# Two-layer attention, gating and scan kernel: normalising on ScalarE, gates by tanh, output rows in chunks, new orders

## The reference, cut to what matters

```python
x = x + attn0(xn) + ffn0(xn)
xn = layernorm(x)
# state-space block, 256 inner channels, 16 states
xs, z = split(xn @ W_in)
xs = silu(causal_conv4(xs) + conv_b)
dt = softplus(xs @ W_dt + b_dt);  Bs = xs @ W_x
h  = h * exp(-A * dt) + Bs            # a scan over the tokens, 16 states
y  = (sum_over_states(h) + D * xs) * silu(z)
x1 = y @ W_out
# feed-forward, 512 hidden
h = silu((xn @ w1.T) * w1_s) * ((xn @ w2.T) * w2_s)
h = gelu((h @ h1.T) * h1_s);  h = gelu((h @ h2.T) * h2_s)
x = x + x1 + (h @ w3.T) * w3_s
```

## Time and profile before

| | |
|---|---|
| runs (3) | 415.56, 415.57 (median), 419.93 us |
| profiled execution | 414.44 us, span 412.5 us |
| granted TensorE clock, mean | 0.983 |
| busy: PE, PEld | 385.6 us (93%), 195.0 us (47%) |
| busy: DVE, ACT, POOL | 302.4 us (73%), 320.5 us (78%), 239.1 us (58%) |
| POOL acc additions, line 1115, x128 | 158.2 us |
| DVE scans, line 1076, x128 | 145.7 us |
| ACT exponentials of line 1019, x128 | 81.6 us |
| chain that ended last | PE 53%, ACT 22%, DVE 13%, issue 9% |

### The profile page before, as it was taken

How to read it: one execution, slowest core, us unless ns; L and a number is a source line. 1 busy time by engine, 2 the same in 40 slices (tenths; PEclk the granted TensorE clock), 3 DMA queues, 4 the chain that set the end, 5 groups by cost and what they waited for, 6 DMA issues and landing times.

```text
span 412.5 us, 5932 instructions
## 1 busy us (share of the span) xinstructions
PE 385.6 (93%) x1864; PEld 195.0 (47%) x1864; DVE 302.4 (73%) x509; ACT 320.5 (78%) x537; POOL 239.1 (58%) x276
## 2 busy tenths in 40 slices
PE   7999999999998999898869898999999999889995
PEld 6875454545544353342213443545446544375445
DVE  5857869687696979226847998788997799978500
ACT  2331668686689868999999999999999999959510
POOL 5233642351423210134398797699997899998640
PEclk9999999999999999999977999999999999989999
DMA  5189556576255220000000000000000000000000
GB/s 188 50 143 196 116 151 151 101 180 100 68 85 113 30 50 2 3 0 2 0 1 0 1 2 0 0 2 25 1 1 2 0 26 1 0 2 25 1 0 27
DMA packets 27679, 19.03 MB, mean 46 GB/s; under 512 B 2816, under 2 KB 26240, under 8 KB 27392
## 3 DMA queue, kind: packets, MB, share of 16 engines
q1 hardware_dynamic: 27648, 18.65, 21.1%
HBM read 13.46 MB, written 4.98 MB: 45 GB/s over the span
## 4 chain that ended last, share of the span: by engine, by line
PE 53%; ACT 22%; DVE 13%; issue 9%; DMA 1%; POOL 1%; SPq 0%; ACTq 0%; POOLq 0%; DVEq 0%
PE bank L852 7%; PE bank L840 6%; DVE hb L1076 6%; PE bank L352 5%; ACT da L1019 5%; PE bank L337 4%; PE bank L323 4%; PE bank L391 3%; PE bank L383 3%; PE bank L911 3%; ACT pt L519 3%; PE bank L445 3%; DVE mx L558 2%; PE bank L829 2%; PE bank L830 2%
## 5 line engine op out<-in xcount | busy, mean ns | idle before, releaser
L1115 POOL TENSOR_TENSOR acc<-acc,hb 128x512 f32<-128x512 f32 x128 | 158.2, 1267 | 35.3 <-DVE hb L1076 25.2
L1076 DVE TENSOR_TENSOR_SCAN hb<-da,bank 128x512 f32<-128x512 f32 x128 | 145.7, 1200 | 32.3 <-PE bank L813 28.7
L558 DVE TENSOR_REDUCE mx<-bank 128x2 f32<-128x512 f32 x128 | 82.5, 682 | 27.1 <-PE bank L323 21.6
L519 ACT ACTIVATE pt<-bank 128x512 f32<-128x512 f32 x128 | 71.0, 597 | 17.3 <-PE bank L337 16.6
L1019 ACT ACTIVATE da<-dt,nega 128x510 f32<-128x510 f32 x128 | 81.6, 710 | 0.2
L852 PE MATMUL bank<-gelu,ld 128*128 128x512 f32 x128 | 58.4, 595 | 2.1 <-ACT gelu L1000 2.1
L840 PE MATMUL bank<-sil,ld 128*128 128x512 f32 x128 | 60.0, 604 | 0.0
L337 PE MATMUL bank<-q_st,k_st 51*128 51x512 bf16 x128 | 43.4, 388 | 5.6 <-ACT pt L519 5.6
L323 PE MATMUL bank<-k_st,q_st 48*128 48x256 bf16 x256 | 43.4, 273 | 2.4 <-DVE mx L558 2.0
L852 PEld LDWEIGHTS bank<-gelu,ld 128*128 128x128 f32 x128 | 23.7, 190 | 30.5 <-issue 26.0
L840 PEld LDWEIGHTS bank<-sil,ld 128*128 128x128 f32 x128 | 24.2, 194 | 27.3 <-issue 26.2
(11 more groups left out here) (132 smaller groups left out, 565.1 us busy)
## 6 DMA issues: line engine op xcount, KB each, us to landing
q_st<-q_scr SPq DMA_DIRECT2D x8, 384.0 KB, 6.3
q_st<-q_scr SPq DMA_DIRECT2D x15, 192.0 KB, 3.9
ld<-in_pack SPq DMA_DIRECT2D x2, 1024.0 KB, 5.6
q_scr<-qk_parts SPq DMA_DIRECT2D x8, 192.0 KB, 2.3
k_st<-k_scr SPq DMA_DIRECT2D x15, 96.0 KB, 4.9
q_scr<-qk_parts SPq DMA_DIRECT2D x8, 128.0 KB, 1.9
out<-x SPq DMA_DIRECT2D x4, 256.0 KB, 2.0
ld<-in_pack SPq DMA_DIRECT2D x1, 968.0 KB, 5.6
```

The lines of the kernel that those rows point to most:

```text
L519: act(pt[:, n % 8, :], st(b, n)[:, :], ACT.Exp, scale=HD ** -0.5).then_inc(p_ok, 1)
L558: eng.tensor_reduce(mx[:, 2 * pair:2 * pair + 2, q], s_bank[n % 2][:, :].rearrange("p (h k) -> p h k", h=2), AX.X, ALU.max).then_inc(mx_ok, 1)
L1076: eng.tensor_tensor_scan(hb[:, s % NPAIR, c, :], da(n).rearrange("p b n -> p (b n)"), b_bank(g, s)[:, :], 0.0, ALU.mult, ALU.add).then_inc ...
L1115: TT(acc[:, g % 2, c, :], acc[:, g % 2, c, :], hb[:, s % NPAIR, c, :], ALU.add).then_inc(add_ok, 1)
```

## The change

Eight edits go together.
- Layer 0 and layer 1 normalise in one ScalarE pass, x * inverse + (-mean * inverse); VectorE makes the product -mean * inverse (`nmr`, `nmean`) after the inverse. Layer 0's `normalised` moves from VectorE to ScalarE. Epsilon is the bias of the square root.
- GpSimd's `biased` adds two tiles at a time.
- `start_acc` moves from ScalarE to GpSimd, one piece for each half.
- silu(u) = u/2 * (1 + tanh(u/2)): z's gate in all four groups (`TANH_Z`), x's gate and the feed-forward's in group 0 only (`TANH_X`, `TANH_FFN`). ScalarE takes tanh, VectorE multiplies by u (`zm`, `xm`, and a second operation in `mul`). The halves go into copies of the constants (`d_half`, `f1_half`, `f12_half`, `wout_half`), made in `decay_rates`, and into the scales of `b_in` and `dt`.
- `out` accumulates the y part of all four token tiles first, then one chunk of the feed-forward product at a time, each with a wait for its own `hid`.
- In the last group the output rows lie in both banks; residual and store are halved in all groups.
- The lists of all five queues are new. SP issues x ahead of the weights.
- 13 of the 96 warm blocks come after the first `A`.

```diff
 deviation0(k):
-    eng.wait_ge(st_mv, 2 * k + 2)
-    act(std[:, lo:hi], t["veps"][:, lo:hi], ACT.Sqrt).then_inc(st_sd, 1)
+    eng.wait_ge(st_mv, k + 1)
+    act(std[:, lo:hi], mv[:, lo:hi, 1], ACT.Sqrt, bias=t["eps"][:, 0:1]).then_inc(st_sd, 1)
+normalised(b):                                   # on ScalarE; VectorE's is removed
+    eng.wait_ge(st_rs, 2 * x_part(b) + 2)
+    reached(eng, xnT_ps, b - 1, 1, 1)
+    for q in range(TPB):
+        c = b * TPB + q
+        last = act(xn[:, q, :], x_sb[:, c, :], ACT.Identity, bias=nmr[:, c:c + 1], scale=rstd[:, c:c + 1])
+    last.then_inc(xn_ok, 1)
 inverse(k):                                      # and the same in layer 1
     eng.reciprocal(rstd[:, lo:hi], std[:, lo:hi]).then_inc(st_rs, 1)
+    eng.wait_ge(st_rs, 2 * k + 1)
+    eng.scalar_tensor_tensor(nmr[:, lo:hi], mv[:, lo:hi, 0], -1.0, rstd[:, lo:hi],
+                             ALU.mult, ALU.mult).then_inc(st_rs, 1)
 normalise(g):
-    act(xn[...], x1[:, c, :], ACT.Identity, bias=nmean[:, c:c + 1])     # four, then
-    act(xn[...], xn[...], ACT.Copy, scale=rstd[:, c:c + 1])             # four
+    act(xn[...], x1[:, c, :], ACT.Identity, bias=nmean[:, c:c + 1], scale=rstd[:, c:c + 1])
...
+TANH_Z, TANH_X, TANH_FFN = (0, 1, 2, 3), (0,), (0,)
 gate_z(g, c):
-    act(zs[:, g % 2, c, :], (pA, pB)[c][:, :], ACT.Silu).then_inc(z_ok, 1)
+    act(zs[:, g % 2, c, :], (pA, pB)[c][:, :], ACT.Tanh, scale=0.5).then_inc(z_ok, 1)
+z_mul(g, c):                                     # VectorE
+    reached(eng, z_ok, g, 2, c + 1)
+    STT(zs[:, g % 2, c, :], zs[:, g % 2, c, :], 1.0, (pA, pB)[c][:, :], ALU.add, ALU.mult).then_inc(zm_ok, 1)
+x_mul(g, c):                                     # VectorE, group 0
+    reached(eng, xs_ok, g, 2, c + 1)
+    STT(xs[:, g % 2, c, :], xs[:, g % 2, c, :], 1.0, xc[:, c, :], ALU.add, ALU.mult).then_inc(xm_ok, 1)
-start_acc(g):                                    # ScalarE
-    act(acc[:, g % 2, c, :], xs[:, g % 2, c, :], ACT.Copy, scale=t["D"][:, c:c + 1])
+start_acc(g, c):                                 # GpSimd
+    x_done(eng, g)
+    eng.tensor_scalar(acc[:, g % 2, c, :], xs[:, g % 2, c, :], d[:, c:c + 1], None, ALU.mult)
...
 out_rows:
-    for k in range(KC):
-        mm(pB[:, r], g3[:, k, r], w3[:, k, :], start=(k == 0), stop=False)
-    for c in range(CI):
-        last = mm(pB[:, r], y[:, c, r], wout[:, c, :], start=False, stop=(c == CI - 1))
+    n == 0: for q, c: mm(out_bank(g, q)[:, r], y[:, c, r], wo[:, c, :], start=..., stop=False)
+    n >= 1: reached(eng, g3_ok, g, KC, k + 1)
+            for q: mm(out_bank(g, q)[:, r], g3[:, k, r], w3[:, k, :], start=False, stop=...)
```

The orders' tails, as an example of how they differ (tensor):

```diff
-        out 2*b 3*second b 3*second b 2*second 2*b 8*third 4*out
+        ffn b ffn b out ffn b ffn b 2*b out out 3*second b 2*second b 2*second b second b 2*out third b 2*third
+        b third b 4*third 6*out
```

More of the change, by code:

```diff
@@ L120 @@
-    gpsimd="""ones 3*biased 8*G 2*qk_split maxima_split 6*G qk_split 2*G constants maxima_split 8*G qk_split maxima_split
-        8*G qk_split maxima_split 8*G qk_split maxima_split 8*G qk_split maxima_split 8*G maxima_split 8*G
-        maxima_split split 6*add split 26*add y 6*add y 13*add split 13*add y 5*add y 14*add split 20*add y
-        3*add y 22*add 2*y""",
+    sync="""x_in constants0 x_in head x_in ffn_weights 3*put fetch stack 3*put fetch put stack 2*put 3*rows fetch loads
+        2*put 3*rows loads put stack fetch rows put 2*rows put stack put fetch 3*rows stack 3*put fetch loads
+        3*rows stack 3*put fetch 3*rows 3*put fetch stack 3*rows stack 3*rows loads 8*out landed""",
@@ L124 @@
+    gpsimd="""ones 2*biased 8*G 2*qk_split maxima_split 8*G qk_split maxima_split 8*G biased maxima_split qk_split 8*G
+        maxima_split constants G qk_split 7*G maxima_split 3*G qk_split 5*G maxima_split qk_split 8*G
+        maxima_split 8*G maxima_split 2*start split 9*add 2*start 9*add split 13*add y 5*add y start 6*add start
+        8*add split 14*add y 4*add y 8*add start 3*add start 7*add split 11*add y 4*add y 26*add y add y""",
 )
@@ L949, in gate_z @@
             reached(eng, y_ok, g - 2, CI, CI)
-            act(zs[:, g % 2, c, :], (pA, pB)[c][:, :], ACT.Silu).then_inc(z_ok, 1)
+            if g in TANH_Z:
+                last = act(zs[:, g % 2, c, :], (pA, pB)[c][:, :], ACT.Tanh, scale=0.5)
+            else:
+                last = act(zs[:, g % 2, c, :], (pA, pB)[c][:, :], ACT.Silu)
+            last.then_inc(z_ok, 1)
         def gate_x(g, c):
@@ L954, in gate_x @@
             reached(eng, dt_ps, g - 2, 2, 2)
-            act(xs[:, g % 2, c, :], xc[:, c, :], ACT.Silu).then_inc(xs_ok, 1)
-        def start_acc(g):
-            reached(eng, xs_ok, g, 2, 2)
-            reached(eng, y_ok, g - 2, CI, CI)
-            for c in range(CI):
-                act(acc[:, g % 2, c, :], xs[:, g % 2, c, :], ACT.Copy,
-                    scale=t["D"][:, c:c + 1]).then_inc(acc_in, 1)
+            if g in TANH_X:
+                last = act(xs[:, g % 2, c, :], xc[:, c, :], ACT.Tanh, scale=0.5)
+            else:
+                last = act(xs[:, g % 2, c, :], xc[:, c, :], ACT.Silu)
+            last.then_inc(xs_ok, 1)
         def normalise(g):
@@ L1012, in decay @@
             if n == 0:
[L1013 removed]
+                settled(eng, i_act, NIA)
             if n == ND0:
@@ L1107, in gpsimd_pieces, with start_acc @@
         TT = eng.tensor_tensor
+        def start_acc(g, c):
+            x_done(eng, g)
+            reached(eng, y_ok, g - 2, CI, CI)
+            settled(eng, i_act, NIA)
+            d = d_half if g in TANH_X else t["D"]
+            eng.tensor_scalar(acc[:, g % 2, c, :], xs[:, g % 2, c, :], d[:, c:c + 1], None, ALU.mult).then_inc(acc_in, 1)
         def add(g, n):
@@ L1148, in constants @@
                               ALU.mult).then_inc(i_pool, 1)
-        return dict(constants=constants, split=split, add=lambda n: add(n // (2 * NS), n % (2 * NS)),
+        return dict(constants=constants, split=split, start=lambda n: start_acc(n // CI, n % CI), add=lambda n: add(n // (2 * NS), n % (2 * NS)),
                     y=lambda n: gated(n // CI, n % CI))
```

277 lines of the change are left out of this document (155 added, 122 removed).

## The result

The changed kernel takes 389.51 us (median of 5 runs, 389.35 to 391.72) against 415.57 us: 0.935 of the kernel before, 95% interval 0.9291 to 0.9408. The direction was right; the forecast had half of the size.

The account below looks back on a forecast made before the run. Start-up, then full TensorE in layer 0, then ScalarE from 160 us, with TensorE at the end, were taken to bound the kernel; -3.0 - 9.0 - 1.6 = -13.6 from 415.57 gives 402.0 us, own range 397 to 407, wider 394.5 to 410.

Parts of the forecast that it names:

- Start-up, -3.0: Kernel start up to the first scores: x issued first, epsilon as bias, normalising on ScalarE; 3.0 us sooner, ends 1 and 5.
- Layer 0, 0 us: Layer 0: ScalarE's added normalising hides behind full TensorE, and the 7.9 us taken off VectorE were in slack; no change.
- Head of layer 1, -3: Up to the second softplus: ScalarE's order has 113.4 against 116.2 us of work, so GpSimd's first addition comes 3 us sooner.
- -10.2: ScalarE between layer 0's fifth batch and layer 1's last x_out: 20 table loads instead of 28, 1.28 us each.
- The discount of 6 us for VectorE's products: ScalarE's stage: 14 new tanh-gate products on VectorE delay TensorE, taking 6 us off the 15.4 us gain.
- start_acc, -3.7 for three pairs: ScalarE's stage: three pairs of starting products leave ScalarE for GpSimd, -3.7 us; 0.8 us each on GpSimd, ends 0.6 and 1.27.
- ScalarE's stage -9.0: Layer 1, where ScalarE is full: fewer loads, start_acc moved, one-pass normalising, less VectorE's products; -9.0 us, ends -3 and -15.
- GpSimd sets the limit: First addition to y(5), group 2's second output product: GpSimd's work bounds the gain; y(5) near 347, span end near 397.
- Rival (a): GpSimd binds: starting product costs 1.27 us, its idle does not shrink, y(5) at 356, end at 408; chance 0.15.
- Rival (b): More comes back: ScalarE's whole 15.4 us and the stretch at clock 0.81; 397 us or lower; chance 0.12.
- Rivals (c) and (d): Tanh shares exp's table but not silu's or gelu's, 51 loads, 404.5, chance 0.08; or needs its own, 66 loads, 420, 0.06.
- Tail, -1.6: Kernel end: y part and first chunks run beside the last gelu, last residual and store halved; 1.6 us less.

## Why the prediction was right in direction and short in size

- **Start-up, -3.0, measured -5.0 at x_in together with layer 0.** The single steps came as written: first scores at 21.67 for "near 22", one pass of 0.88 us for 0.86 (only the small product ahead of it took 0.64 us for 0.2). The step that failed is "Layer 0, 0 us": VectorE is "rid of 7.9 us, also in slack". It is not in slack between the first scores and the first A: layer 0's normalising on VectorE costs 5.6 us, 3.2 of them there and 2.0 between the first A and x_in. Of SP's new order only 1.8 are seen, and those not clear of noise. The rule that I had read from the earlier trace rows for 60:90, where TensorE is full, did not hold for 25:50.
- **Head of layer 1, -3 by "113.4 against 116.2 us of work", measured -8.6.** This is the largest error. ScalarE's work was added up from the first instruction, over layer 0, where it waits for TensorE anyway, so the sum says little of the stretch from x_in on. Counted from x_in the kernel before has seven loads ahead of the first softplus (161.94 to 180.60), the changed one its softplus load alone (168.56): 6 x 1.28 = 7.7 us. The run with group 0's gates by silu, which has eight more loads than the changed kernel ahead of the first addition and eight products fewer, gives back 6.3 of the 8.6. The count should have begun where ScalarE begins to be late.
- **A load at 1.28 us, the stage's price per load.** By the medians the stage lost 1.74 us a load (two silu operations that serve nothing), 1.74 (group 0's gates: 12.5 and the 3.2 us of eight products, over nine) and 2.0 (group 1: 5.6 and 2.4, over four); by the traces 1.5, 1.6 and 2.1. The term "-10.2" for eight loads would be 12 to 14 at these prices, as an estimate: they come from loads put in, and the two loads taken out of group 1 brought nothing. Each load also stops TensorE, which ScalarE then waits for.
- **The discount of 6 us for VectorE's products: about right.** 14 operations, 5.6 us by the medians, 4.6 by the trace.
- **start_acc, -3.7 for three pairs: 2.5 for all four.** GpSimd's product took 1.56 us, above my upper end of 1.27, and it did not matter.
- **ScalarE's stage -9.0 (ends -3, -15), measured -15.0.** With the medians' prices it is 13.9 + 2.5 + 3.4 (one-pass normalising, taken from the forecast, not tried alone) - 1.9 - 5.6 = 12.3; with the traces' prices it is half a microsecond to one less. Some 3 us are open, and 4 to 5 against the kernels without the stretch at half clock (16.3 us). The clock (10.2 us at half clock from 212 us on in the profiled execution of before, 3.4 in that of after) and the new orders are candidates that no run parts.
- **"GpSimd sets the limit": wrong.** Rival (a) had 0.15 and lost; GpSimd relieved brought nothing, and 32 matmuls in TensorE's queue cost 0.20 to 0.22 us each. Between the first addition and y(5) GpSimd's idle time did fall, to 14.7 us (forecast 14) from 23.8, but that was not what bounded the end. A row at 20.0 of 20 did not make the engine the limit.
- **Rival (b), 0.12, "397 or lower", was what happened,** in part for a reason that it did not have: of its two, ScalarE's whole 15.4 us is near the truth; what the stretch at clock 0.81 was worth is not shown. The forecast's y(5) at 347 came within 5 us (342.1) and its 14 us of idle time within 1, by an argument that the runs refuse: that was luck.
- **Rivals (c) and (d)** fell with the 47 loads. The Trainium skill lists tanh with exp and with sigmoid and names no silu table (ScalarE: Activation LUTs, Table sets: the hidden batching unit); here tanh needs no load behind silu either, and behind gelu it was not tried.
- **Tail, -1.6: -2.6** behind y(5). The whole edit is worth 3.9: some 0.5 us behind the last y, as the term meant it, and the rest further ahead, which the forecast had at nothing.
- **The difference of 1.1 us between profile and median** had the other sign after: 391.72 profiled, 389.51 median. That is 3.3 us of the 12.5 missed, and no error of mechanism; the stretch at half clock (1.4 us) and the later start (up to 1.2) account for most of the changed kernel's part.

## What to carry to other kernels

Add up an engine's work from the point at which it becomes the late one, not from the start: a difference ahead of that point can vanish in waits, and one behind it counts. Where two engines feed each other in turns, an instruction put into one can cost more than it lasts (1.5 to 1.7 us for a 1.28 us load), and one taken out can bring nothing if its successors then wait. Look for slack stretch by stretch: a row of 60 to 90 us said nothing of VectorE between 25 and 50. An engine that is full in its windows need not be the limit; take 5 us off it, or put 7 us on its neighbour, before you argue from it.
